# Keeping x in a ring of six tiles instead of loading it twice, and zeroing from a tile a third as large

## The reference, cut to what matters

```python
def _layernorm(x, eps=1e-05): return (x - mean(x)) / sqrt(var(x) + eps)       # over the last axis

x = x + xattn(_layernorm(x), ctx, ctx, w_q, w_k, w_v, w_o)   # x: (16, 256, 256); 16 heads of 16, causal
x = x + ffn(_layernorm(x), ...)                              # three fast-feedforward trees (q, k, v), then attention

def _fff(x, node_w, node_b, w1, b1, w2, b2):   # one tree: 4 binary decisions pick one of 16 leaves for each token
    hidden = relu(x @ w1[leaf] + b1[leaf])     # 256 -> 64
    return hidden @ w2[leaf] + b2[leaf]        # 64 -> 256
```

## Time and profile before

| | |
|---|---|
| median of 3 runs | 658.51 us (652.58 to 661.08) |
| span of the profiled execution, first to last instruction | 656.6 us |
| PE busy in it | 587.3 us (89%) |
| DVE busy | 450.4 us (69%) |
| DMA: bytes, packets | 169.58 MB, 99639 |
| mean granted TensorE clock | 0.951 |

### The profile page before, as it was taken

How to read it: one execution, slowest core, us unless ns; L and a number is a source line. 1 busy time by engine, 2 the same in 40 slices (tenths; PEclk the granted TensorE clock), 3 DMA queues, 4 the chain that set the end, 5 groups by cost and what they waited for, 6 DMA issues and landing times.

```text
span 656.6 us, 14722 instructions
## 1 busy us (share of the span) xinstructions
PE 587.3 (89%) x5119; PEld 500.4 (76%) x5119; DVE 450.4 (69%) x1511; ACT 294.5 (45%) x482; POOL 236.8 (36%) x298
## 2 busy tenths in 40 slices
PE   7588999999999999999998988849998888789996
PEld 6467787887888787788887866738887777579995
DVE  2765676998899899989888765664645544046664
ACT  3104444454545454454444452018876667333331
POOL 5700010133324233432423144413006665565642
PEclk8858999999999999999999897869999999899999
DMA  6798797889989989989977479759999998666763
GB/s 190 230 295 249 230 256 207 272 274 259 274 283 308 230 271 291 276 250 280 306 218 239 146 221 291 213 196 323 355 368 380 365 380 321 211 184 184 197 183 128
DMA packets 99639, 169.58 MB, mean 258 GB/s; under 512 B 12848, under 2 KB 67824, under 8 KB 99568
## 3 DMA queue, kind: packets, MB, share of 16 engines
q1 hardware_dynamic: 87712, 141.83, 69.2%
q0 software_dynamic: 9216, 25.18, 12.7%
q10 hardware_dynamic: 2640, 1.65, 0.9%
HBM read 92.59 MB, written 75.50 MB: 256 GB/s over the span
## 4 chain that ended last, share of the span: by engine, by line
PE 48%; DVE 14%; DMA 13%; SPq 11%; issue 8%; ACT 3%; another core or an unknown queue 2%; ACTq 1%; DVEq 0%; POOL 0%; POOLq 0%
PE banks L820 4%; PE banks L831 4%; DMA parts_dram<-k_lo 4%; DVE mneg L1188 4%; PE banks L846 4%; PE banks L892 4%; SPq L335 4%; PE banks L544 3%; DMA k<-parts_dram 3%; PE banks L913 3%; PE banks L529 3%; PE banks L556 3%; DMA xb<-xs_dram 3%; PE banks L686 3%; PE banks L716 2%
## 5 line engine op out<-in xcount | busy, mean ns | idle before, releaser
L1550 POOL DMA_INDIRECT xs_dram<-xn2s,place x96 | 95.3, 993 | 186.3 <-ACT pt L946 141.2
L946 ACT ACTIVATE pt<-banks 128x768 f32<-128x768 f32 x128 | 103.7, 811 | 102.8 <-PE banks L557 83.3
L1188 DVE TENSOR_REDUCE mneg<-banks 128x2 f32<-128x512 f32 x240 | 122.0, 549 | 34.9 <-PE banks L545 29.0
L544 PE MATMUL banks<-k,q 107*128 107x256 f32 x240 | 76.5, 370 | 15.9 <-DVE mneg L1188 9.6
L556 PE MATMUL banks<-q,k 109*128 109x256 f32 x256 | 75.0, 345 | 2.3 <-ACT pt L946 0.4
L544 PEld LDWEIGHTS banks<-k,q 107*128 107x128 f32 x240 | 46.5, 194 | 27.6 <-DVE mneg L1188 12.4
L557 PE MATMUL banks<-q,k 109*128 109x128 f32 x256 | 57.7, 225 | 0.0
L572 PE MATMUL banks<-pt,vp 128*32 128x256 f32 (+1 forms) x1024 | 56.4, 339 | 0.0
L556 PEld LDWEIGHTS banks<-q,k 109*128 109x128 f32 x256 | 49.1, 192 | 7.7 <-ACT pt L946 6.7
L545 PE MATMUL banks<-k,q 107*128 107x128 f32 x240 | 54.4, 227 | 0.0
L1537 POOL TENSOR_SCALAR ve<-mv 128x2 f32<-128x2 f32 x32 | 7.3, 228 | 127.5 <-DVE mv L1114 81.5
(11 more groups left out here) (177 smaller groups left out, 1301.7 us busy)
## 6 DMA issues: line engine op xcount, KB each, us to landing
ys_dram<-yb SPq DMA_DIRECT2D x36, 512.0 KB
xb<-xs_dram SPq DMA_DIRECT2D x35, 512.0 KB
k<-parts_dram SPq DMA_DIRECT2D x128, 128.0 KB, 4.5
q<-parts_dram SPq DMA_DIRECT2D x64, 256.0 KB, 4.3
xs_dram<-zero SPq DMA_DIRECT2D x45, 256.0 KB
xs_dram<-zero SPq DMA_DIRECT2D x18, 384.0 KB, 4.5
tables<-leafw SPq DMA_DIRECT2D x16, 257.0 KB
xt<-x SPq DMA_DIRECT2D x16, 256.0 KB
```

The lines of the kernel that those rows point to most:

```text
L544: mm(ps[:, 0:S], q[0:KN, t, P:S], k[0:KN, t, :], start=True, stop=True)
L946: nc.scalar.activation(pt[:, 2 * p:2 * p + 2, :], st_banks(b, p)[:, :, 0:S + P], ACT.Exp, scale=SC).then_inc(exp_sb, 1)
L1188: last = nc.vector.tensor_reduce(mneg[1 - u][:, t, 2 * j:2 * j + 2], S_BANKS[:, :, cols], axis=AX.X, op=ALU.max, negate=True)
L1550: gp.indirect_dma_start(xs_dram[tree], bass.IndirectOffsetOnAxis(ap=place[:, k:k + 1], axis=0), xn2s[m % RING][:, t, :], None).then_inc(sc ...
```

## The change

The tiles `xr` and the second load are gone. `xt` has six tiles instead of two, batch b uses tile b % 6, and the residual of batch b-2 reads the tile that the layer norm read. `load_x` now also waits until the residual has read what the tile held. The tile of zeros has one row of 256 in each partition instead of three, and `zero_pages` reads this row two or three times (a broadcast with step 0). In step 16 SP waits for `var2` before it issues the zeros.

```diff
+XR = 6
-        xt = [at(f"xt{i}", [P, T, D]) for i in range(2)]
...
-        xr = [at(f"xr{i}", [P, T, D]) for i in range(2)]
+        xt = [at(f"xt{i}", [P, T, D]) for i in range(XR)]
...
-        b2raw, zero = at("b2raw", [P, TREES, D]), at("zero", [P, 3 * D])
+        b2raw, zero = at("b2raw", [P, TREES, D]), at("zero", [P, D])
...
             def load_x(b, s):
 
                 ge(sp, xn_done, T * (b - 1))
-                sp.dma_start(xt[s][:], x[bass.ds(b * S, S), :].rearrange("(t p) d -> p t d", p=P)).then_inc(x_in[s], 16)
+                ge(sp, x1_sb, b - XR + 1)
+                sp.dma_start(xt[b % XR][:], x[bass.ds(b * S, S), :].rearrange("(t p) d -> p t d", p=P)).then_inc(x_in[s], 16)
...
-            def load_xr(b, s):
-
-                ge(sp, x1_sb, b - 1)
-                sp.dma_start(xr[s][:], x[bass.ds(b * S, S), :].rearrange("(t p) d -> p t d", p=P)).then_inc(xr_in[s], 16)
...
                 for tree in range(TREES):
                     sp.dma_start(by_page(xs_dram[tree])[:, zero_from(b):zero_from(b + 1), :],
-                                 zero[:, 0:k * D].rearrange("p (r d) -> p r d", d=D)).then_inc(done, 16)
+                                 zero[:].unsqueeze(1).to_broadcast([P, k, D])).then_inc(done, 16)
...
+                if b == NB:
+                    sp.wait_ge(var2, NB - 1)
                 if b <= NB:
                     zero_pages(b)
                 if b == NB + 1:
                     zero_after(b + 1)
-                if has(b, -1):
-                    load_xr(b - 1, 1 - u)
...
             def residual(b, n, u):
 
                 v.wait_ge(wo_ps, b - 1)
-                v.wait_ge(xr_in[u], 16 * n)
                 ge(v, x1_out[u], 16 * (n - 1))
                 ge(v, xn2_sb, T * (b - 2))
                 nc.vector.tensor_tensor(x1[u][:].rearrange("p t d -> p (t d)"), G7[:],
-                                        xr[u][:].rearrange("p t d -> p (t d)"), ALU.add).then_inc(x1_sb, 1)
+                                        xt[(b - 2) % XR][:].rearrange("p t d -> p (t d)"), ALU.add).then_inc(x1_sb, 1)
```

More of the change, by code:

```diff
@@ L195, in build @@
         wt_late = sems("wt_late", TREES)
-        x_in, c_in, xr_in = sems("x_in"), sems("c_in"), sems("xr_in")
+        x_in, c_in = sems("x_in"), sems("c_in")
         zeroed_first, zeroed = sem("zeroed_first"), sems("zeroed")
@@ L1108, in norm_in @@
                 for t in range(T):
-                    nc.vector.bn_stats(st1[:, t, :], xt[s][:, t, :]).then_inc(stats1, 1)
+                    nc.vector.bn_stats(st1[:, t, :], xt[b % XR][:, t, :]).then_inc(stats1, 1)
                 v.wait_ge(stats1, T * (b + 1))
@@ L1120, in norm_out @@
                 for t in range(T):
-                    nc.vector.tensor_scalar(xn[s][:, t, :], xt[s][:, t, :], mv1[:, t, 0:1], rs1[:, t:t + 1],
+                    nc.vector.tensor_scalar(xn[s][:, t, :], xt[b % XR][:, t, :], mv1[:, t, 0:1], rs1[:, t:t + 1],
                                             ALU.subtract, ALU.mult).then_inc(xn_done, 1)
```

## The result

The changed kernel takes 653.97 us at the median of 20 runs (650.88 to 657.67), the kernel before 657.65 us in its 20 runs beside them (652.58 to 662.84). The ratio of the runs is 0.9946, with a 95% interval of 0.9922 to 0.9969: a gain of 0.5%, clear of zero and far under the 2% that one would call faster. The profiled execution has a span of 652.5 us against 656.6 us.

The account below looks back on a forecast made before the run. PE was taken as the bound, busy 304.99 of 318 us in stage 1. Span 656.6 - 4.0 us of k-stack stalls = 652.6 us; with the runs' median 1.9 us above span, 654.5 us, range 647.5 to 661 us.

Parts of the forecast that it names:

- The place of the gain: Stage 1, 60 to 378 us: PE's stalls for the k stacks, 4.0 us in matmuls and 7.3 us in weight loads, mostly go.
- The size: Stage 1: 4.0 us gained by PE, from 3.3 us at a relief of 0.7 us to 4.0 us at 1.4 us.
- Which relief counts: At a k stack in stage 1: SP's issue 0.69 us, the engines' bytes 0.72 us; at least one, at most both, 1.4 us.
- The landing of a k stack: k stacks take 4.5 us to land at the median, 2.9 us at least; up to 1.6 us is queueing that less traffic shortens.
- The price of a packet: DMA engines: 55 ns per 1 KB packet, 6 ns of it fixed; xr's removal saves 0.87 us a step, cut zeros cost 0.15.
- The issue of the zeros: SP's issue of the zeros from a repeated row stays near 585 ns: added cost 0, other end 1.75 us.
- the fourth rival: SP pays for the zeros' pieces: slower if each issue costs 0.23 us more, +7.5 us at twice the time; chance 0.06.
- The wait in step 16: SP waits for `var2` until 399.04 us; issues behind it move about 4 us but are caught up: cost 0, scatter margin 1.3 us.
- Stalls that come back as waits for DVE or ACT: Stage 1: removed stalls return as other waits or the next transfer fills the place; gain 0 to 1 us; chance 0.24.
- More tied to the transfers than the waits say: Stage 1: both reliefs at every step, capped by PE's 13.0 us of idle time; gain 8 to 13 us; chance 0.12.
- A worse end of stage 1: End of stage 1: delayed last scatters or one more half-speed clock stretch lose 1 to 4 us; chance 0.08.
- The run's level: Whole run: the median of the runs lies 1.9 us above the profiled span, so 652.6 us of span becomes 654.5 us.

Follow-up runs that it names:

- the pieces alone: Kernel before with only the one-row tile of zeros, read two or three times by each store; x still loaded twice: ratio to before 1.0029, 12 periods 273.30 us.
- the controls: Changed kernel run again without further edits, beside the follow-up kernels: ratios to before 0.9965 and 0.9878, 12 periods 269.35 and 268.61 us.
- bytes back: Changed kernel with the store of x1 writing its tile twice in one transfer, 512 KB instead of 256 KB: ratio to before 1.0015, 12 periods 271.05 us.
- the kernel without further loads: Changed kernel without loads of x from batch 6 and of the context from batch 2 on, reusing old data: ratio to before 0.9880, 12 periods 269.34 us.
- groups 1 and 3: Sets of four follow-up kernels on one chip, each with the changed kernel run again: its ratio to before was 0.9965 in the first, 0.9878 in the other.

## Why the prediction was right

The forecast was 654.5 us in a range of 647.5 to 661 us, and a gain of 4.0 us by shorter stalls. The median is 653.97 us, 3.7 us under that of before. The place and the size of the gain came out; the working behind the size is only in part borne out.

*The place of the gain.* It was put on the stalls for the k stacks, and there it is. The sum of the periods was to be about 268.5 us and is 268.92 us, 269.35 and 268.61 us. The stalls were to fall under 1 and 3 us; they fell to 1.4 and 2.2 us in the first profile, but in another they were still 3.5 and 4.5 us, and in the third none and 1.5 us. That part was too hopeful.

*The size.* 4.0 us, against 3.55 us in the periods of the two first profiles. All five profiles together give 273.16 us (mean of two) against 268.96 us (mean of three), 4.2 us.

*Which relief counts.* I gave SP's issue and the bytes 0.7 us each and let them count singly or together. Put back alone, the issue cost nothing, the bytes 1.7 us in the periods, both together 5.2 us; two small issues without the bytes cost 3.35 us. So neither relief of 0.7 us is worth a fixed share, and the working, which let either one alone win 3.3 us, isn't borne out for the issue. What fits all four is a slack: a little more work on SP's queue is free, and when the slack is used up the k stacks come late. That is an argument from these four kernels; the slack itself wasn't measured. The relief of 0.72 us by the bytes is of the size of what SP's wait for k's unload lost, 0.5 us in a step.

*The landing of a k stack* was read from the earlier trace rows with 6.1 us as the longest. The chain in the earlier trace rows has one of 7.20 us from its issue, so that row doesn't hold every stack. The medians, from which the relief was bounded, stay as they are.

*The price of a packet* (6 ns each, from two queues' averages) led to a packet count of 105,900, against 105,655. The difference is 256 small packets that went with the loads and that I hadn't counted. The kernel with the pieces alone has the 10368 packets more and periods within the scatter of before, so the statement of the Trainium skill (DMA: Bandwidth & Descriptors, Specifications) that transfers run at line rate from 512 bytes up is not contradicted by pieces of 1 KB. What the cutting does cost is seen in SP's issue, of which that statement doesn't speak.

*The issue of the zeros* was taken as unchanged by way of the x load's row. That term of the working, put at 0, was mis-sized: 632 ns against 585 in the first profile, and up to 693 in the controls, 0.14 to 0.32 us in a step. It stayed under the 0.23 us for each store from which the fourth rival decides, so there was a rest of the gain. Why the x load's row was a poor witness isn't isolated. Its pieces are alike and its source doesn't repeat, but repetition alone isn't shown to cost either: the store of x1 takes 732 ns where its source repeats ("bytes back") and 712 to 718 ns where it doesn't.

*The wait in step 16* behaved as worked out: POOL releases it, the last six zeros end before the last residual, no cost shows.

*The rivals.* Stalls that come back as waits for DVE or ACT: refuted by the periods, which fell by as much as was forecast. The waits alone would not decide it, since DVE's wait for the scores was 19.6 and 20.3 us before and 16.6, 21.9 and 16.5 us after. More tied to the transfers than the waits say: refuted for the twelve periods by the kernel without further loads, whose periods stay at the floor; outside them it stays open. The idle time of PE, 13.0 us, was a bound that could never be reached: the changed kernel still idles 10.8 us in the same 318 us, and only 1.4 us of that are stalls for stacks. Slower through the pieces: the sign was right, the size too small. A worse end of stage 1: not seen.

*The run's level.* Adding 1.9 us to the span fitted: the profiled execution of the changed kernel has its own time, 654.33 us, 1.8 us above its span. That the median fell within 0.6 us of the forecast is partly luck: in groups 1 and 3 the changed kernel's medians were 658.1 and 654.96 us, and those of the kernel before 660.9 and 661.25 us.

## What to carry to other kernels

When transfers feed the critical engine through a single queue, price what is removed by the engine's stalls for those transfers, not by the bytes: 4.2 MB less were worth 4 us where 4 to 6 us of stalls hung on them, and 512 KB less in each step after that won nothing in the twelve periods. Find the shortest step without a stall first; what the other steps take beyond it is all that can be won. And don't price a queue's issue time as so much for each issue: here the first added issue was free, and two cost 3 us.

## What was unexpected about the hardware

The time that SP needs to issue a transfer isn't fixed by its shape. The zeros as 128x2x256 from one repeated row took 615 to 756 ns at the median in ten profiles, against 569 to 585 ns as 128x512 (four profiles). But the store of x1, as 128x2x256 too and without any repetition, took 607 to 740 ns in eleven profiles, and the same store behind two small loads 447 ns, never more than 459. The load of x for the layer norm took 588 to 594 ns in the three profiles with two tiles, 540 ns in all nine with six, and 519 to 520 ns in the two with five, for the same bytes and the same shape. What sets these times, pieces, repetition or what stands ahead in the queue, isn't isolated. The number of packets does follow the pieces: 10368 more for the same bytes.

Behind the last residual the two kernels run the same code, and still their five profiles took 244.6 to 248.2 us there. One profile can show a change of 0.5% in this kernel only in a stretch where nothing else moves, here the twelve periods at a granted clock of 1.00; the whole time shows it only over many runs, as the 20 and 20 above.
